# Five batches sorted by expert in blocks of 128 rows, results scattered back by row numbers, and no key projection

## The reference

```
# tok: two convolutions, layer norm, a small feed-forward, layer norm, max over 3 neighbours -> 373 tokens
h = silu(conv1(x)); h = silu(conv3(h)); y = layer_norm(conv1(h) + x)
y = layer_norm(gelu(y @ w_ff1.T + b) @ w_ff2.T + b + y); h = maxpool3(y)
# attention, one head of 128, on the normed h
xn = layernorm(h); q = (xn @ Wq + bq) * 128**-0.5; k = xn @ Wk + bk
h = h + softmax(q @ k.T) @ xn
# mixture of 8 experts, two per token
xf = layernorm(h); gate = softmax(relu(xf @ gw1 + gb1) @ gw2 + gb2)
top_w, top_idx = top_k(gate, 2); top_w = softmax(top_w)      # combine[t, e], zero but for two e
for e in range(8):                                            # hidden size 256
    out += combine[:, e] * (gelu(xf @ we1[e] + be1[e]) @ we2[e] + be2[e])
return h + out
```

## Time and profile before

| | |
|---|---|
| median of 3 runs | 247.51 us (247.3 to 248.34) |
| profiled execution, whole | 247.55 us |
| profiled execution, span | 245.6 us |
| blocks of 256 rows | 19, T to L2 from about 154 to 196 us |
| (batch, expert) units done densely | 32 |
| transfers | 35.57 MB, 15.4 MB of them the fill with zeros |

### The profile page before, as it was taken

The page is one execution under the profiler, slowest core; times in us unless marked ns, Lnnn a source line. Parts: engine busy times, 40 slices in busy tenths (PEclk is TensorE's granted clock), DMA queues, the critical chain, the costliest instruction groups (busy, mean ns, idle before and its releaser), DMA issues.

```text
span 245.6 us, 5357 instructions
## 1 busy us (share of the span) xinstructions
PE 234.1 (95%) x1651; PEld 185.3 (75%) x1651; DVE 156.2 (64%) x663; ACT 144.4 (59%) x292; POOL 114.3 (47%) x185
## 2 busy tenths in 40 slices
...
GB/s 150 242 249 308 371 411 414 410 412 415 215 0 4 0 0 4 1 3 31 32 42 77 43 44 93 102 107 264 263 313 205 44 68 61 74 45 107 73 32 65
DMA packets 23127, 35.57 MB, mean 145 GB/s; under 512 B 5345, under 2 KB 17324, under 8 KB 23100
## 3 DMA queue, kind: packets, MB, share of 16 engines
...
HBM read 10.28 MB, written 21.28 MB: 128 GB/s over the span
## 4 chain that ended last, share of the span: by engine, by line
PE 80%; DVE 12%; issue 3%; ACTq 2%; ACT 2%; DVEq 0%
PE PS L1148 16%; PE PS L1141 16%; PE PS L1173 7%; PE PS L1164 7%; PE PS L1066 6%; PE PS L1084 5%; PE PS L956 3%; PE PS L1073 3%; DVE stat L672 2%; PE PS L1056 2%; PE PS L1060 2%; PE PS L1157 2%; PE PS L1031 2%; PE PS L1033 2%; PE PS L985 1%
## 5 line engine op out<-in xcount | busy, mean ns | idle before, releaser
L640 ACT ACTIVATE gd<-PS,bias 128x373 f32<-128x373 f32 x64 | 35.0, 572 | 28.9 <-PE PS L1141 27.0
L1148 PEld LDWEIGHTS PS<-w_all,gd 128*125 128x125 f32 x384 | 44.8, 187 | 4.2 <-ACT gd L640 0.7
L1148 PE MATMUL PS<-w_all,gd 128*125 128x128 f32 x384 | 46.3, 273 | 0.0
L1141 PE MATMUL PS<-xt_sb,w_all 128*128 128x373 f32 x128 | 46.0, 482 | 0.1
L513 POOL DMA_INDIRECT yg<-ys,pos_x x24 | 29.3, 1219 | 19.6 <-issue 19.3
L883 DVE SCALAR_TENSOR_TENSOR x_sb<-PS,comb,x_sb 125x128 f32<-125x128 f32 x84 | 24.3, 347 | 17.4 <-PE PS L1148 16.4
L467 POOL TENSOR_TENSOR ve<-mv,eps 125x3 f32<-125x3 f32 x32 | 6.2, 194 | 57.8 <-DVE mv L676 57.4
L492 POOL DMA_INDIRECT xs<-xn,pos_x x24 | 29.0, 1207 | 7.9 <-issue 6.7
L1141 PEld LDWEIGHTS PS<-xt_sb,w_all 128*128 128x128 f32 x128 | 21.4, 190 | 10.9 <-issue 4.3
L469 POOL TENSOR_TENSOR rstd<-ve,mhalf 125x3 f32<-125x3 f32 x32 | 27.5, 860 | 2.5
L1084 PEld LDWEIGHTS PS<-xn,prob_t 125*125 125x125 f32 (+1 forms) x144 | 16.8, 187 | 1.6 <-issue 0.7
(11 more groups left out here) (180 smaller groups left out, 461.3 us busy)
## 6 DMA issues: line engine op xcount, KB each, us to landing
...
blk_w<-w_all POOLq DMA_DIRECT2D x11, 321.0 KB, 3.1
...
```

The costliest lines, as they stand in the source:

```text
L640: act.activation(gd[:, k % GD, c, 0:TP], of("D1", n)[:, 0:TP], ACT.Gelu, bias=bias128[:, 2 + k % E * HC + c:3 + k % E * HC + c]).then_inc( ...
L1141: pe.matmul(f[:, 0:TP], w_all[:, k % E, c * 128:(c + 1) * 128], x32[:, DENSE[k // E], 0:TP], start=True, stop=True).then_inc(S["D1"], 1)
L1148: last = pe.matmul(f[0:P, j * D:(j + 1) * D], gd[:, n % GD, c, OFF[j]:OFF[j] + P], w_all[:, n % E, H + c * D:H + (c + 1) * D], start=(c == ...
```

## The change

Five batches (1 to 5) are sorted and three (0, 6, 7) are dense. Blocks have 128 rows: 8 with a fixed place and 29 dynamic, 37 in all. A row of `xs` has 129 numbers: the 128 features and the row of `ys` that its result belongs to. POOL writes these numbers at the start into `rows_x`, of which `l4` fills the features for the first choice; SP copies them for the second (`c4`). A place that no token takes holds a number outside `ys`. A block's results are scattered by POOL to `ys` (`so`), with that number as index; results out of bounds are dropped. `ys` is thus in token order and SP reads it with plain loads (`yl`). `ys` is not filled; `xs` is, 9.9 MB. SP issues the weight loads `lw` too, with 7 slots, 10 slots for rows and 6 for results.

Keys: since softmax does not see what is constant per query, scores are computed as (xn @ N + c) @ xn.T, with N made once from Wq and Wk (`ft` transposes both, `fn` multiplies them); `bk` and `k_t` go, and `xn_t` gets 1 added, which the sums in `ft` undo. The output is written from `h2` itself; `da` and `fin` no longer write to `ob`. The start of the queues differs: ACT issues only the loads that its first work needs, the x loads go to SP, wk, wq and the biases to POOL. `WARM` is (11, 6, 6, 6, 4, 2, 2, 4, 2, 3), 46 products. Semaphores count what an engine has done instead of even and odd batches.

All five orders are new. What they hold of the pieces spoken of, counted on PE in five stretches, before -> after:

| piece | up to rk.1 | rk.1 to rk.2 | rk.2 to T.0 | T.0 to last L2 | behind it |
|---|---|---|---|---|---|
| D1 | 9 -> 4 | 10 -> 6 | 11 -> 8 | 1 -> 20 | 33 -> 10 |
| D2 | 3 -> 0 | 5 -> 3 | 7 -> 5 | 0 -> 8 | 17 -> 8 |
| bk | 6 -> 0 | 2 -> 0 | | | |
| ct, bd | 2, 2 -> 1, 0 | 0, 0 -> 0, 1 | | 0, 0 -> 2, 2 | 2, 2 -> 0, 0 |
| at, pt, sc, a7 | 5, 15, 18, 8 -> 4, 12, 17, 7 | 1, 3, 3, 0 -> 2, 6, 3, 1 | 2, 6, 3, 0 -> 2, 6, 4, 0 | | |
| rk, ft, fn | 0, 0, 0 -> 1, 1, 1 | 1, 0, 0 -> 1, 0, 0 | 1, 0, 0 -> 1, 0, 0 | | |
| warm products | 23 -> 46 | | | | |
| T, L1, L2 | | | | 19 -> 37 each | |

DVE up to rk.1: a4 3 -> 1, a7 2 -> 1, at 5 -> 4, b1 2 -> 1, bd 2 -> 0, bq 2 -> 1, da 3 -> 0, hv 0 -> 4, l2 3 -> 1, mp 4 -> 3, pt 5 -> 0, sc 18 -> 16, rk 0 -> 1, ft and fn 0 -> 1. DVE from rk.1 to rk.2: at 1 -> 2, bd 0 -> 1, da 4 -> 1, mp 0 -> 1, pt 1 -> 4, sc 2 -> 3, b1 and bq change places.

```diff
-GROUPS = ((2, 3, 4, 5),)
+SPARSE = [1, 2, 3, 4, 5]
-BLK = 256
+BLK = 128
-SLOTS = 6
-YBUF = 4
+XW = D + 1
+SLOTS = 10
+WSLOTS = 7
+YBUF = 6
+YG = 3
 PE_ORDER, around the last blocks and behind them:
+L1.27 D2.13:4 L1.28 L2.25 T.30 D2.14 L2.26 L2.27 L1.29 D1.31 L2.28 L1.30 T.31 T.32 D1.32 L2.29 T.33 L1.31 L2.30 bd.2
+L1.32 L2.31 T.34 D1.33 L1.33 T.35 D1.34 L1.34 T.36 L2.32 L2.33 D2.15 L1.35 L2.34 D1.35 L1.36 L2.35 D1.36 D1.37 L2.36
+D2.16 D1.38 D2.17 D1.39 ... D2.20 D2.21 D1.47 D2.22 D2.23
 DVE_ORDER, its end:
+yv.35 bd.2 yv.36 da.15 da.16 da.17 da.18 fin.0 fin.1 fin.2 da.19 da.20 fin.3 da.21 da.22 da.23 fin.4
 SP_ORDER:
+c4.1 c4.2 c4.3 c4.5 c4.4 lx.0 lx.1 lx.2 lw.8 lw.9 lx.3 lx.4 lx.5 lx.6 lw.10 lx.7 lw.11 lx.8 lw.12 lx.9 lx.10 lw.13
+lx.11 lx.12 lw.14 lx.13 lx.14 lw.15 ... lw.34 lx.34 lx.35 lw.35 lw.36 lx.36 od.0 yl.0 yl.1 yl.2 out.0 yl.3 out.1 ...
 POOL_ORDER:
-... scat.23 p4.6 p4.7 lw.8 ... lw.18 gat.0 ... gat.23
+... scat.29 p4.6 p4.7 so.0 so.1 ... so.36
 in sync:
+                if name == "c4":
+                    k = SPARSE.index(n)
+                    wait_nth(sp, "xn4", n)
...
+                        sp.dma_start(rows_x[lo:hi, k, 1, :, 0:D], rows_x[lo:hi, k, 0, :, 0:D]).then_inc(s_copy[k % 2], 16)
                 if name == "lx":
+                    if n == 0:
+                        sp.wait_ge(s_scat, 16 * NI * NS)
+                    if n == E:
+                        wait(sp, "tab", 1)
+                    wait_so(sp, n - SLOTS)
+                    row = CAP * n if n < E else sp.value_load(tab_x[0:1, n - E:n - E + 1], ...)
+                    sp.dma_start(blk_x[i][:], xs[bass.ds(row, BLK), :].rearrange("(p t) d -> p t d", t=NT))\
+                        .then_inc(s_bx[i], 16)
+                if name == "lw":
+                    k = n - E
...
+                    if k >= WSLOTS:
+                        wait(sp, "yv", n + 1 - WSLOTS)
+                    e = sp.value_load(tab_e[0:1, k:k + 1], min_val=0, max_val=E - 1)
+                    sp.dma_start(blk_w[k % WSLOTS][:], w_all[:, bass.ds(e, 1), :].rearrange("p o d -> p (o d)"))\
+                        .then_inc(s_bw[k % WSLOTS], 16)
+                if name == "yl":
+                    if n == 0:
+                        for m in range(NB - YBUF, NB):
+                            wait_so(sp, m)
+                    if n >= YG:
+                        wait(sp, "ob", n - YG + 1)
+                    for lo, hi in SPLIT:
+                        sp.dma_start(yg[lo:hi, n % YG, :, :], ys[2 * T * n:2 * T * (n + 1), :]...)
 in gpsimd:
+                if name == "so":
+                    wait(pool, "yv", n + 1)
+                    for t in range(NT):
+                        pool.indirect_dma_start(ys, bass.IndirectOffsetOnAxis(
+                            ap=blk_x[n % SLOTS][:, t, D:XW].bitcast(u32), axis=0),
+                            yblk[n % YBUF][:, t, :], None, bounds_check=ROWS_Y - 1, oob_is_err=False)
 in vector:
+                if name == "ft":
...
+                    link(dve.tensor_reduce(sums[:], f[:, 0:2 * D].rearrange("e (w i) -> e w i", w=2), AX.X, ALU.add))
+                    dve.tensor_scalar(wqt[:], f[:, D:2 * D], SCALE, None, ALU.mult)
+                    dve.tensor_scalar(shift[:, 1:2], sums[:, 1:2], bias128[:, 0:1], -SCALE, ALU.subtract, ALU.mult)
+                    link(dve.tensor_scalar(shift[:, 0:1], sums[:, 0:1], bias128[:, 1:2], -1.0 / D, ALU.subtract, ALU.mult))
+                    dve.tensor_scalar(wkt[:], f[:, 0:D], shift[:, 0:1], None, ALU.add).then_inc(S["fd"], 1)
                 if name == "yv":
-                    wait_for(dve, s_ys[n % YBUF], 16 * (n // YBUF))
+                    wait_so(dve, n - YBUF)
 in tensor:
-                if name == "bk":
-                    wait_nth(pe, "xnt", n)
-                    f = claim(name, n, nth("k", n))
-                    pe.matmul(f[:, 0:TP], wk_sb[:], xn_t[:, s, :], start=True, stop=True).then_inc(S["kp"], 1)
+                if name == "fn":
...
+                    pe.matmul(f[:, 0:D], wqt[:], wkt[:], start=True, stop=True)
+                    pe.matmul(f[:, D:D + 1], wkt[:], shift[:, 1:2], start=True, stop=True).then_inc(S["ft"], 1)
```

More of the change, by code:

```diff
@@ L41 @@
 DPAIRS = sorted({n // 2 for n in DENSE})
+ITEMS = {q: [i for i in range(NI) if 2 * q + i % 2 in SPARSE] for q in SPAIRS}
 GD = 3
-PAIRS = [sorted({n // 2 for n in ns}) for ns in GROUPS]
-BLK = 256
+BLK = 128
 NT = BLK // 128
-NDYN = [2 * T * len(ns) // BLK for ns in GROUPS]
-NBLK = [E + n for n in NDYN]
-FIRST = [sum(NBLK[:g]) for g in range(NG)]
-NB = sum(NBLK)
-BLOCK_OF = [(g, b) for g in range(NG) for b in range(NBLK[g])]
-CAP = [-(-T * len(ns) // BLK) * BLK for ns in GROUPS]
-SPARE = [E * c for c in CAP]
@@ L138, in pieces, with ranks @@
         yield name, int(n)
-WARM = (6, 2, 2, 5, 1, 2, 3, 2)
+WARM = (11, 6, 6, 6, 4, 2, 2, 4, 2, 3)
 ON_ACT = set(pieces(ACT_ORDER))
+EVICT = {"n1": "l1", "n2": "l2", "xn3": "l3", "xn4": "l4", "yt": "a4", "y2": "a7", "h": "hv", "xnt": "b1", "q": "bq",
+         "x32": "h1", "pt0d": "pt0", "pt1d": "pt1", "pt2d": "pt2", "xT": "xT", "ctr": "ct"}
+def ranks(order):
+    seen, rank = {}, {}
+    for name, n in pieces(order):
+        rank[name, n] = seen[name] = seen.get(name, 0) + 1
+    return rank
+RANK_ACT, RANK_DVE = ranks(ACT_ORDER), ranks(DVE_ORDER)
 BANK = {tuple(word.split(":")[0].split(".")): int(word.split(":")[1]) for word in PE_ORDER.split()}
@@ L317, in wait, with nth, normed_by, wait_so @@
                 eng.wait_ge(S[name], value)
+        def nth(name, n):
+            piece = EVICT[name], n
+            return (name + "_act", RANK_ACT[piece]) if piece in ON_ACT else (name + "_dve", RANK_DVE[piece])
         def wait_nth(eng, name, n):
             if n >= 0:
-                eng.wait_ge(S[name + str(n % 2)], n // 2 + 1)
-        def nth(name, n):
-            return name + str(n % 2), n // 2 + 1
-        def wait_for(eng, s, value):
-            if value > 0:
-                eng.wait_ge(s, value)
-        def loads(n):
-            return sum(BLOCK_OF[m][1] >= E for m in range(n % SLOTS, n + 1, SLOTS))
+                wait(eng, *nth(name, n))
+        def normed_by(i, n):
+            return sum(4 if (f"l{i + 1}", m) in ON_ACT else 2 for m in range(n))
+        def wait_so(eng, n):
+            if n >= 0:
+                eng.wait_ge(s_so[n % YBUF], 16 * NT * (n // YBUF + 1))
         def tiles(ap):
             return [ap[:, j, :] for j in range(NJ)]
+        def weights(eng, n):
+            if n < E:
+                eng.wait_ge(S["be1"], 1)
+                return w_all[:, n, :]
+            eng.wait_ge(s_bw[(n - E) % WSLOTS], 16 * ((n - E) // WSLOTS + 1))
+            return blk_w[(n - E) % WSLOTS][:]
+        def xn4_of(n):
+            if n in SPARSE:
+                return [rows_x[:, SPARSE.index(n), 0, j, 0:D] for j in range(NJ)]
+            return tiles(xn4[:, DENSE.index(n), :, :])
         def flat(ap):
@@ L378, in _ @@
             sp.dma_start(be2_sb[:], be2).then_inc(S["wt"], 16)
-            sp.wait_ge(S["zinit"], 1)
-            for g in range(NG):
-                per = (SPARE[g] + BLK * (1 + NDYN[g])) // 128
-                n = max(k for k in range(1, ZN + 1) if per % k == 0)
-                for rows in (xs[g], ys[g]):
-                    sp.dma_start(rows.rearrange("(p r q) d -> p r (q d)", p=128, q=n),
-                                 zeros[:, 0:n * D].unsqueeze(1).broadcast_to([128, per // n, n * D])).then_inc(s_zero[g], 16)
```

541 lines of the change are left out of this document (261 added, 280 removed).

## The result

The changed kernel takes **250.12 us** (median of 4 runs, 249.99 to 251.19) beside 247.93 for the kernel before in the same runs: 1.0092 of its time, interval 1.0071 to 1.0114. It is 0.9% slower; the forecast was 237 and 4% faster, and the time lies outside the range (224 to 247). The same kernel was timed three times more on other chips, each time beside the kernel before: 1.0326 [1.0286, 1.0366], 1.0293 [1.0243, 1.0344] and 1.0184 [1.0118, 1.0251]. The size of the loss depends on the chip, its sign does not.

A forecast was written before the change was run, and what follows sets the result against it. PE bound most of the kernel, with DVE close behind in the front; T.0 at 141, 70 for blocks paced by SP's loads, 24 of tail and 1.95 around the span gave 237 us, range 224 to 247.

The forecast's parts named there:

- Front: Start to first T: DVE-bound to rk.1 at 93, rk.2 at 117, then the scatter chain, T.0 at 141 us.
- this pitch: Scatters before the first T: they start 1.49 us apart, unslowed by a busy DVE.
- warm-ups mostly hide: Front: most of the 46 warm-up products fall in DVE's gaps; all in the way would be +7.4 us.
- the first block load: Before T.0: PE waits 1 to 3 us for it, since the scatter chain outlasts PE's work.
- lx.10 waits for the first block's scatter to land: Blocks: landing at 149, then 50 loads at 1.09 us on SP, lx.36 issued at 203.5, stretch 70 us.
- PE's own count has T.36 at 141 + 59.3: Blocks: by PE's work alone the last T comes at 200.3 us; SP's loads make it 5 us late.
- SP is hidden: Rival, blocks: SP's loads take 0.9 us or less, stretch 65, time 232 us; chance 19%.
- PE only: Rival, whole kernel: PE stays the only bound everywhere, T.0 at 134, time 223 us; chance 12%.
- POOL paces: Rival, blocks: scatters at a pitch of 2.0 us make the stretch 77.4, time 244 us; chance 9%.
- SP's queue in full: Rival, lx.10 to lx.36: 1.4 us per load, time 253 us, no gain from 1.30 on; chance 10%.
- The tail: Behind the last L2: DVE, not PE, ends it, with 24 us to the last output.

The follow-up runs named there:

- hoist24_warm: The changed kernel with 24 row and 24 expert numbers read before the first dynamic load, and 20 warm-up products instead of 46: 257.19 us, 1.0326 of the kernel before.
- batch4: The changed kernel, but SP reads the numbers of four loads with one instruction: 253.4 us, 0.9961 of the kernel before.
- no_lw: The changed kernel without the 29 weight loads and their number reads, blocks using resident weights: 250.48 us, 0.9898 of the kernel before.
- lw_pool: The changed kernel with 12 of the 29 weight loads back on POOL: 248.78 us, 0.9972 of the kernel before; again 248.08, 0.9951.
- pool_hoist: The changed kernel with 12 weight loads on POOL and 18 of SP's remaining numbers read ahead: 249.74 us, 0.9891 of the kernel before.

## Why the prediction was wrong

**Front: right to 2 us.** rk.1 came at 95.2 (93 forecast), rk.2 23.8 us behind it (24), the first T 24.2 behind that (23.7): 143.3 instead of 141. The scatters kept their pitch of 1.49, but for one gap of 1.66, and the last started at 137.4, 17.1 us behind the last CAST of pos_x. The prediction held this pitch against the rule on what DVE and GpSimd share (the Trainium skill, "SBUF — State Buffer", section "Who interferes with whom"), which speaks of DVE instructions with two SBUF inputs or in a two-port mode. The trace tests that rule only weakly: of the 16.7 us for which DVE was busy in those 24.5, some 1.4 were instructions with both inputs in SBUF (L892, L934, L938, L942, L945), the longer gap lies where L942 and L945 ran (131.1 to 132.2), and the rows don't tell the mode of the others. That warm-ups mostly hide was right (hoist24_warm).

One thing in the front came out for another reason than forecast. PE was to wait 1 to 3 us for the first block load; it waited for none. That load was issued at 140.6, and PE, which had waited 0.7 us for a copy on ACT, came from two D1 to the first T at 143.3. PE and the load were ready within a us of each other, so the time of the first T is partly luck. On the other chips the changed kernel's first T was at 146.1 to 147.7, with lx.0 issued at 142.3 to 142.4: there PE itself was late. I can't say why.

**The step that failed: "lx.10 waits for the first block's scatter to land, at ... 149. Behind it are 50 more lx and lw", at 1.09 us each.** That SP's queue paces the blocks was right; how long it takes was not: it took 75.7 us from lx.0 to lx.36, where the forecast had 64.7. Both halves of the term were off.
- lx.10 waited for no scatter; it was late by SP's own queue. Ahead of it stand 8 static row loads, five weight loads and two dynamic row loads, which I never summed. By my own prices that is 8 x 0.36 + 7 x 1.09 = 10.5 us, and lx.10's own read before its issue 0.7: with lx.0 at 138.8, lx.10 at 150.0, so the missing sum alone is 1 us. It took 14.6, from 140.6 to 155.2, since the static loads cost 0.50 each and the seven others 1.40. lx.10 was 6.2 us late: 1.8 from the front, 1.0 from the missing sum, 3.4 from dearer loads. The scatter would have held it too, if less: it started at 149.1, 5.8 us behind the first T instead of 3.4, and by the median of 2.4 us to landing was down at about 151.5 (an estimate).
- The 50 loads behind it took 61.1 us, 1.22 each instead of 1.09: 6.6 us. The register work was as read (0.15), but the three other parts were all off. The number read was cheaper (0.27 to 0.28, not 0.47: 9.5 us less over 50 loads), a weight load's issue is 0.50, where I had used a block load's 0.36 for both (3.4 us more), and the small steps and gaps between come to about 0.35, not 0.1 (12.5 us more). That my 1.09 came within 12% is partly luck: a read taken too dear hid most of the gaps.

Together 12.8 us, as lx.36 shows: issued at 216.3 instead of 203.5. The last T to the last L2 took 6.9 instead of 5.4; counted piece by piece from PE_ORDER at the prediction's own prices it is 6.5 (five L2, two L1, three D1, a D2 and the T), so 1.1 of this was a slip of the sum. The rest follows: 2.3 + 10.3 (first T to last T, 75.0 against 64.7) + 1.5 - 0.8 (tail 23.2, not 24) = 13.3, and 235.1 + 13.3 = 248.4, the span.

**"PE's own count has T.36 at 141 + 59.3": wrong too, and hidden by the first error.** T, L1 and L2 cost what I said (0.11, 0.44 to 0.45 and 0.45 in starts that follow each other), yet with SP relieved the first T to the last is 68.5 to 72.2 us, not 59.3 (58.1, with the slip above put right), in all ten kernels that relieve SP of reads or of weight loads and keep the 128-row blocks, batch4 excepted. My price for the blocks came from back-to-back rows and held only for work that stays back to back.

Why it doesn't stay so is argued, not shown. PE's pieces were halved, the steps of ACT and DVE were not: before, a block's gelu took 0.94 us (two of 0.47) beside an L2 of 0.90 that could cover it; now it takes 0.73 (two of 0.37) beside an L2 of 0.45. But no_lw's waits put little on the gelu itself (gb_t, 1.1 of the 7.4 us). The three longest are single ones: for ACT's copy of a transposed block (2.4), for an eviction on DVE (2.3), and for the transposed gate weights that a bd needs (comb_t, 1.4). So the places of a few pieces in the hand-written orders are as good a suspect as the size of the blocks, and no run changed them alone.

From the first T to the last my forecast thus had two wrong terms: SP's queue makes it 75 to 78 us instead of 64.7, and what stands behind SP is about 70 us instead of 59.3.

**The rivals.** "SP is hidden" is refuted for the changed kernel; and if it had been hidden, the time would be near the kernel before's, as lw_pool and no_lw show, not 232. "PE only" and "POOL paces": no; POOL's scatters started 1.27 us apart where nothing held them, and POOL waited 40.7 us for evictions (L951). "SP's queue in full" named the mechanism and the place, with T waiting for loads to the end, but put the point of no gain at 1.30 us per load. The loads came at 1.22, and the gain was already gone, since the queue started 6 us late. Its 10% was too little: its evidence, had pairs 1.13 and 1.39 apart, the mean of which is 1.26.

**The tail** was right: DVE ends it, with the second part of fin.4 (answers to the earlier trace rows).

```profile
241.21 2.86 DVE L923 SCALAR_TENSOR_TENSOR x_sb<-PS,comb,x_sb 125x128 f32<-125x128 f32 x9
...
244.89 0.88 DVE L964 SCALAR_TENSOR_TENSOR x_sb<-yg,w_top,acc 125x128 f32<-125x128 f32 x3
```

**Where the expected gain went.** 26.8 us less PE work became: about 7 us in SP's queue (by three comparisons, each on one chip: lw_pool 7.2, no_lw 7.2, pool_hoist 7.9), about 12 us of waits, lower clock and gaps in the block stretch (70 for 58.1), and the rest in a front and a tail that DVE and the scatters set. The first is shown by undoing; the second by what is left when loads are gone, though no run shortened it. A run that shortens the scatter chain before the first T wasn't made.
